# Cross-attention and a quantised FFN on one core: two stages with folded values against one unrolled pipeline without the fold

## What is computed

```python
def reference(x, ctx, proj_q, bias_q, proj_k, bias_k, proj_v, bias_v, w_out, w_gate, w_up, w_down):
    xn = layernorm(x)
    q = einsum('bnd,hdk->bhnk', xn, proj_q) + bias_q          # 16 heads of 64
    k = einsum('bnd,hdk->bhnk', ctx, proj_k) + bias_k
    v = einsum('bnd,hdv->bhnv', ctx, proj_v) + bias_v
    attn = softmax(einsum('bhqk,bhnk->bhqn', q, k) / 8)       # 154 columns a head
    hid = transpose(einsum('bhqn,bhnv->bhqv', attn, v))       # 1024 values a row
    x = x + hid @ w_out.T
    z = layernorm(x)
    h = silu(fp4_linear(z, w_gate)) * fp4_linear(z, w_up)     # 704 values a row
    return x + fp4_linear(h, w_down)

def fp4_quant_dequant(x):          # both operands of each fp4_linear, in blocks of 16
    scale = max(max(abs(block)) / 6, 1e-12)
    return grid_round(block / scale) * scale     # grid 0, .5, 1, 1.5, 2, 3, 4, 6 with sign
```

## Time and profile before

| | us |
|---|---|
| median of 3 runs | 482.89 (482.14 to 484.28) |
| span of the profiled execution, first to last instruction | 480.2 |
| TensorE matmul busy | 399.3 (83%) |
| VectorE busy | 410.6 (85%) |
| ScalarE busy | 283.6 (59%) |
| GpSimd busy | 232.4 (48%) |

### The profile page before, as it was taken

One profiled execution on the slowest core, in us unless ns is written; L12 is line 12 of the kernel. 1 busy time (PEld: TensorE's weight loads), 2 busy tenths in 40 slices (PEclk: granted clock), 3 DMA queues, 4 the chain that ended last, 5 costly groups with the idle time before them and its releaser, 6 DMA issues.

```text
span 480.2 us, 10222 instructions
## 1 busy us (share of the span) xinstructions
PE 399.3 (83%) x3581; PEld 308.9 (64%) x3581; DVE 410.6 (85%) x789; ACT 283.6 (59%) x862; POOL 232.4 (48%) x177
## 2 busy tenths in 40 slices
PE   1889769979989989799799899995687687696965
PEld 1668548858768768587687687883355464464753
DVE  2799886996987988979969879779989999989993
ACT  3597558757756677487577677755344554533641
POOL 7330133253352542542523523423877888768872
PEclk9999979999989999999999999998698998988999
DMA  7940000000000000000000000000000000000001
GB/s 244 315 175 1 2 0 1 2 2 1 1 0 0 0 0 0 0 0 0 0 0 0 1 0 1 1 1 1 1 0 1 23 11 11 22 11 11 23 13 54
DMA packets 8406, 11.18 MB, mean 23 GB/s; under 512 B 499, under 2 KB 6335, under 8 KB 8383
## 3 DMA queue, kind: packets, MB, share of 16 engines
q1 hardware_dynamic: 8383, 10.88, 7.1%
HBM read 8.78 MB, written 2.10 MB: 23 GB/s over the span
## 4 chain that ended last, share of the span: by engine, by line
DVE 52%; PE 29%; issue 9%; ACT 7%; DMA 1%; DVEq 1%; SPq 0%; POOLq 0%; POOL 0%; ACTq 0%
PE ps L356 8%; PE ps L357 7%; PE ps L358 7%; DVE arena L958 5%; DVE negmax L919 5%; PE ps L456 3%; DVE xn L869 3%; DVE arena L931 3%; DVE arena L910 3%; PE ps L448 3%; DVE vw L864 2%; DVE arena L1087 2%; DVE arena L1126 2%; DVE arena L975 2%; DVE arena L969 2%
## 5 line engine op out<-in xcount | busy, mean ns | idle before, releaser
L1178 POOL TENSOR_TENSOR arena<-arena,rinv 128x616 f32<-128x616 f32 x64 | 77.7, 1214 | 174.0 <-DVE rinv L927 174.0
L676 ACT ACTIVATE arena<-ps,ebias 128x154 f32<-128x154 f32 x256 | 96.2, 397 | 37.9 <-DVE ebias L922 37.5
L356 PE MATMUL ps<-vw,arena 128*128 128x256 f16 (+1 forms) x352 | 98.1, 279 | 24.0 <-DVE xs L939 10.7
L357 PE MATMUL ps<-vw,arena 128*128 128x256 f16 (+1 forms) x352 | 97.8, 278 | 0.0
L358 PE MATMUL ps<-vw,arena 128*128 128x256 f16 (+1 forms) x352 | 97.7, 278 | 0.0
L356 PE MATMUL ps<-arena,xnT_h 128*128 128x352 f16 x128 | 46.0, 359 | 27.0 <-DVE xnT_l L1009 25.6
L686 ACT ACTIVATE arena<-ps 128x512 f16<-128x512 f32 x80 | 48.4, 605 | 32.9 <-PE ps L456 32.3
L931 DVE TENSOR_TENSOR arena<-ps,arena 128x512 f16<-128x512 f32 x80 | 54.0, 675 | 8.4 <-ACT arena L686 7.8
L356 PEld LDWEIGHTS ps<-vw,arena 128*128 128x128 f16 x352 | 34.7, 99 | 33.8 <-DVE arena L931 20.3
L676 ACT ACTIVATION_READ_ACCUMULATOR arena<-ps,ebias 128x1 f32 x256 | 54.8, 214 | 0.0
L919 DVE TENSOR_REDUCE negmax<-ps 128x4 f32<-128x616 f32 x64 | 50.6, 790 | 2.9 <-PE ps L448 1.6
(11 more groups left out here) (136 smaller groups left out, 1033.1 us busy)
## 6 DMA issues: line engine op xcount, KB each, us to landing
out_dram<-arena SPq DMA_DIRECT2D x16, 128.0 KB, 1.7
xs<-in_x_dram SPq DMA_DIRECT2D x2, 896.0 KB, 10.1
arena<-in_L_xattn_w_out_dram SPq DMA_DIRECT2D x1, 1024.0 KB, 6.4
wffn<-in_L_ffn_w_down_dram SPq DMA_DIRECT2D x1, 704.0 KB, 8.0
wffn<-in_L_ffn_w_gate_dram SPq DMA_DIRECT2D x1, 640.0 KB, 11.0
wffn<-in_L_ffn_w_up_dram SPq DMA_DIRECT2D x1, 640.0 KB, 5.5
vw<-in_ctx_dram SPq DMA_DIRECT2D x1, 308.0 KB
xs<-in_x_dram SPq DMA_DIRECT2D x2, 128.0 KB, 5.0
```

The source lines that it names most:

```text
L356: pe.matmul(o, a_h, b_h, start=start, stop=False)
L357: pe.matmul(o, a_h, b_l, start=False, stop=False)
L676: last = act.activation(prob[:, s, h * L:(h + 1) * L], ps[:, 2 * (j % 2) + k % 2, (k // 2) * L:(k // 2 + 1) * L], ACT.Exp, bias=ebias[:, s ...
L1178: pool.tensor_tensor(v, v, rinv[:, s, 4 * j:4 * j + 4].unsqueeze(2).to_broadcast([P, 4, L]), ALU.mult).then_inc(normed, 1)
```

## The change

The change rewrites the kernel. Keys, queries, scores and the two-part products remain. What differs:

- There is no fold. Values stay as `v_h`, `v_l` (128 context rows) and the 26 rows left are kept for four heads together in `vl_h`, `vl_l`. For each unit of two tiles `mix` forms the transposed head outputs with 96 matmuls of 256 columns, whose outputs take 64 partitions each and alternate between the two halves; they are split into `hidT_h` and `hidT_l`, and `project` multiplies them by w_out (48 matmuls).
- Attention and FFN of a unit run in one pipeline of 11 steps of 8 slots, written out in full. In step s the scores, exponentials and transposes of unit s, the queries of unit s + 1, the head outputs of unit s - 1, the input quantiser and gate/up of unit s - 2, and the second hidden quantiser and down projection of unit s - 3 are issued. Units 0 to 7 exist.
- PSUM has three rings of two: banks 0 to 3 for scores and gate/up, banks 4, 5 for transposes, banks 6, 7 for queries, head outputs, projections and down.
- The quantiser has five passes: value (GpSimd), magnitude (one ScalarE `Abs`), two VectorE passes of `max` with add and subtract, scale (GpSimd).
- SiLU is `tanh` and a scaled copy on ScalarE, a VectorE pass with the up half, and a product on GpSimd (`gated`).
- The key is scaled beforehand, so that the row maximum is the bias of the exponential directly. The layernorm of x runs on ScalarE, the Newton steps of the inverse root on GpSimd in a chain of 14 small instructions; the result and x are added on VectorE.

The diff, cut to what the texts speak of (`unit(u)` is true for 0 to 7; `turned`, `grouped`, `s_bank`, `m_bank`, `t_bank` wait for and select a bank):

```diff
-            def fold(n):
...
+            def mix(u, j):
+                b = batch(2 * u)
+                pe.wait_ge(t_low, T_AT[("p", 2 * u + 1, 4)] + 1)
+                o = next_group(("pv", u, j))
+                for i in range(2):
+                    for n, (vh, vr, part) in enumerate(((v_h, vl_h, 0), (v_l, vl_l, 0), (v_h, vl_h, 1))):
+                        for r in range(2):
+                            h = 4 * j + 2 * i + r
+                            pe.matmul(o[r * DK:(r + 1) * DK, i * 256:(i + 1) * 256], vh[:, b, h * DK:(h + 1) * DK],
+                                      pT[:, u % 2, part, h], start=n == 0, stop=False)
+                        for r in range(2):
+                            last = pe.matmul(o[r * DK:(r + 1) * DK, i * 256:(i + 1) * 256], vr[:, b, j, 2 * i + r],
+                                             pT[:, u % 2, part, H + j], start=False, stop=n == 2)
+                last.then_inc(m_mm, 1)
...
+            def next_use(job):
...
+                if n >= 2:
+                    kind, i = S_ORDER[n - 2]
+                    if kind == "score":
+                        pe.wait_ge(exp_done, i + 1)
+                    else:
+                        pe.wait_ge(gu_act, i + 1)
+                        pe.wait_ge(gu_done, i + 1)
...
+            for step in range(STEPS):
+                for kk in range(8):
+                    k = 8 * step + kk
+                    if unit(step): score(k)
+                    if 0 <= k - 2 < 4 * TILES:
...
+                        turn_p(k - 2)
+                    if kk == 0:
+                        if unit(step - 2): project(step - 2, 1)
+                        if unit(step + 1): turn_x(step + 1)
+                        if unit(step - 3): turn_h(2 * (step - 3))
+                    if kk == 1:
+                        if unit(step - 3): down(2 * (step - 3))
+                        if unit(step + 1): query(step + 1, 0)
+                    if kk in (2, 3):
+                        if unit(step - 1): mix(step - 1, kk - 2)
+                        if kk == 3 and unit(step - 3): turn_h(2 * (step - 3) + 1)
+                        if unit(step + 1): query(step + 1, kk - 1)
+                    if kk == 4:
+                        if unit(step - 2): turn_xq(step - 2)
+                        if unit(step - 2): gate_up(4 * (step - 2))
+                        if unit(step - 3): down(2 * (step - 3) + 1)
+                    if kk in (5, 6):
+                        if unit(step - 1): mix(step - 1, kk - 3)
+                        if unit(step - 2): gate_up(4 * (step - 2) + kk - 4)
+                        if kk == 6 and unit(step + 1): query(step + 1, 3)
+                    if kk == 7:
+                        if unit(step - 2): gate_up(4 * (step - 2) + 3)
+                        if unit(step - 1): project(step - 1, 0)
...
+            def exps(k):
+                t, j = k // 4, k % 4
+                o = s_bank(("score", k))
+                act.wait_ge(max_done, k + 1)
...
+            def gate_act(g):
...
+                act.activation(act_h[t % 2][:, at], ps[:, o, 0:GU], ACT.Tanh, scale=0.5 / FS).then_inc(tanh_done, 1)
+                act.activation(gate[t % 2][:, at], ps[:, o, 0:GU], ACT.Copy, scale=0.5 / (FS * FS)).then_inc(gu_act, 1)
...
+                    if 0 <= k - 2 < 4 * TILES:
+                        p_high((k - 2) // 4, (k - 2) % 4)
...
+                    if unit(step): exps(k)
...
+                    if kk == 4 and unit(step - 2):
+                        xq_high(step - 2)
+                        gate_act(4 * (step - 2))
...
+                    if kk == 7 and unit(step - 2): gate_act(4 * (step - 2) + 3)
...
+                    if kk == 1 and unit(step - 3): magnitude(2 * (step - 3) + 1, hvalued, *tmp[1], hmagic)
+                    if kk == 7 and unit(step - 2): magnitude(2 * (step - 2), hvalued, *tmp[0], hmagic)
...
+            def to_grid(v, a, s, chain, done):
...
+                after(dve.scalar_tensor_tensor(v, a, 1.5 * GRID, v, ALU.max, ALU.add), s, chain)
+                dve.scalar_tensor_tensor(v, a, 1.5 * GRID, v, ALU.max, ALU.subtract).then_inc(done, 1)
...
+                    if unit(step): row_max(k)
...
+                    if kk == 0 and unit(step - 3): up_act(4 * (step - 3) + 3)
+                    if kk == 1 and unit(step - 2): add_attention(step - 2)
+                    if kk == 2 and unit(step + 1): q_low(step + 1, 0)
...
+                    if kk == 7 and unit(step + 1): q_low(step + 1, 3)
+                    if kk == 7 and unit(step - 2): up_act(4 * (step - 2) + 2)
...
+                    if 0 <= k - 2 < 4 * TILES:
+                        p_low((k - 2) // 4, (k - 2) % 4)
...
+                    if kk == 4 and unit(step - 2):
+                        xq_low(step - 2)
+                        up_act(4 * (step - 2))
+                    if kk in (5, 6) and unit(step - 1): hid_low(step - 1, kk - 3)
+                    if unit(step): inverse(k)
...
+                    if kk == 0 and unit(step - 3): scales_h(2 * (step - 3) + 1)
+                    if kk == 1 and unit(step - 3): grid_h(2 * (step - 3) + 1)
+                    if kk == 2 and unit(step - 2): scales_x(step - 2)
+                    if kk == 3 and unit(step - 2): grid_x(step - 2)
+                    if kk == 6 and unit(step - 2): scales_h(2 * (step - 2))
+                    if kk == 7 and unit(step - 2): grid_h(2 * (step - 2))
...
+            def gated(t):
+                pool.wait_ge(gu_done, 2 * t + 2)
+                pool.wait_ge(gu_act, 2 * t + 2)
+                pool.tensor_tensor(act_h[t % 2], act_h[t % 2], gate[t % 2], ALU.mult).then_inc(hid_ready, 1)
...
+                    if 0 <= k - 1 < 4 * TILES: norm(k - 1)
+                    if kk == 0:
+                        if unit(step - 3): round_h(2 * (step - 3))
+                        if unit(step - 3): gated(2 * (step - 3) + 1)
+                    if kk == 1:
+                        if unit(step - 3): value_h(2 * (step - 3) + 1)
+                        if unit(step - 2): norm_2(step - 2)
+                    if kk == 2 and unit(step - 3): round_h(2 * (step - 3) + 1)
+                    if kk == 3 and unit(step - 2):
+                        value_x(step - 2)
+                        round_x(step - 2)
+                    if kk == 6 and unit(step - 2):
+                        gated(2 * (step - 2))
+                        value_h(2 * (step - 2))
```

More of the change, by code:

```diff
@@ L66, in peeled @@
[L66 to L98 removed]
+WT_JOBS = [("w1", c, j) for c in range(KC) for j in range(0, W1T, 4)] + [("wd", 0, j) for j in range(0, FC, 2)]
@@ new lines, in scored_in @@
+def scored_in(step, kk):
+    if unit(step): yield ("score", 8 * step + kk)
+    if kk >= 4 and unit(step - 2): yield ("gu", 4 * (step - 2) + kk - 4)
+SLOTS = [(step, kk) for step in range(STEPS) for kk in range(8)]
+T_ORDER = [("bias",), ("ctx", 0), ("ctx", 1), ("x", 0)] + [j for s in SLOTS for j in turned_in(*s)]
+M_ORDER = [("q", 0, j) for j in range(QUADS)] + [j for s in SLOTS for j in mixed_in(*s)]
+S_ORDER = [j for s in SLOTS for j in scored_in(*s)]
+T_AT = {j: n for n, j in enumerate(T_ORDER)}
@@ new lines, in project @@
+            def project(u, s):
+                if s == 0:
+                    pe.wait_ge(m_done, M_AT[("pv", u, QUADS - 1)] + 1)
+                    o = next_group(("proj", u))
+                else:
+                    o = m_bank(("proj", u))
+                for p in range(PAIRS):
+                    last = three(o[:, s * D:(s + 1) * D], hidT_h[:, p, s * P:(s + 1) * P], hidT_l[:, p, s * P:(s + 1) * P],
+                                 wo_h[:, p], wo_l[:, p], p == 0, p == PAIRS - 1)
+                if s == 1: last.then_inc(m_mm, 1)
@@ L1150, in _ @@
-            steps(dve, ffn, first=2, last=STEPS - 2)
-            for t in range(2 * STEPS - 2, 2 * STEPS):
-                h_low(*step_of(t))
+                dve.wait_ge(wk_high, c + 1)
+                dve.scalar_tensor_tensor(heads_of(wk_l, c), by_chunk(raw_k)[:, c], WS, heads_of(wk_h, c),
+                                         ALU.mult, ALU.subtract).then_inc(wk_low, 1)
+            dve.wait_ge(ld_x0, 16)
+            norm_stats(0, 4)
+            norm_guess(0, 4)
+            x_low(0)
```

1690 lines of the change are left out of this document (780 added, 910 removed).

## The result

The changed kernel takes 575.5 us (median of 4 runs, 573.9 to 580.0) against 482.8 for the kernel before in the same comparison: a ratio of 1.191, 95% interval 1.184 to 1.197. The forecast was 545 us, slower. The direction and the likeliest case held, and the time lies in the range; the point was 30 us too low.

What follows compares the result with a forecast made beforehand. It took each slot's chain of in-order handovers to bound the kernel, not one engine's work. Set-up 46, steps 0 to 2 138, steps 3 to 6 219, step 7 51 and drain 92 made 546, given as 545 us; range 500 to 580.

Steps and rivals of the forecast that it cites:

- What bounds: Unit of two tiles: three engines have 36 to 39 us of work; whether in-order handovers hide is the question.
- Faster by overlap: Whole kernel: engines overlap as well as now, a unit takes 43.4 us, the whole 461; chance 0.15.
- the tie at 47: Middle of the loop: the two kernels tie when a unit takes near 47 us; chance 0.04.
- Slots: Middle step: the chains of slots 0 to 7, 4.9 to 8.4 us each, laid end to end make 54.7 us.
- a rival at 0.10: Whole kernel: unpaired `mix` adds 32 us and a fallen TensorE clock 14, together 591; chance 0.10.
- Step 2: Pipeline step with no final part and nine weight turns, priced at 51 us.
- The drain: Steps 8, 9 and 10, which empty the pipeline, priced at 39, 36 and 17 us.
- `mix` on halves: Head outputs on TensorE: matmuls alternating between array halves run in pairs, 5.2 us a unit.
- The other bound: Head outputs on TensorE: matmuls do not pair, 10.5 us a unit, about 4 us more a unit, 32 in all.
- Newton on GpSimd: Slot 1: 14 small instructions at 0.4 us each, 5.6 us, ending before `normal_x1` is due.
- Table loads: ScalarE: a load at each change between exponential and tanh adds 82 us, 627 in all; chance 0.03.
- What would show it: Changed profile: middle steps about 55 us, VectorE near 75% busy, waiting longest for tanh, magnitude and last transposes; one table load.

Runs made afterwards that it cites:

- the run that keeps the clock up: Changed kernel plus 22 unused matmuls in slot 4, 12 before the transposes and 10 behind them: 557.1 us, 1.151 against the kernel before.

## Why the prediction was right, and where it was short

**What bounds.** Right. The forecast said that three engines have 36 to 39 us of work in a unit and that handovers in order decide. Measured were 35.9 (VectorE), 32.8 (ScalarE) and 43.3 of latencies (TensorE) in 54.7. The added statistics passes, which cost nothing, and `down` moved, which gave 9 us without removing an instruction, show for slot 4 that the order and not the amount sets it; the other slots rest on their timelines. VectorE's sum of durations was 39.1, and the durations in that step add to 38.7; the busy time is 35.9, since each instruction's record overlaps the next by some 0.08 us. The forecast set a sum of durations against 45.0 of busy time; the sign of the result did not hang on it.

**Faster by overlap.** Fell. It needed slots 4, 7 and 0 under 6 us; they are 10.0, 7.4 and 8.5. The loop runs at 54.7, well above the tie at 47.

**Slots.** Five of eight within 0.5 us, and the sum exact, but by luck, because slots 1, 2, 3 and 7, priced 2.1 us too long together, cover slots 0 and 4, 2.1 too short. The failing step is the one that said of slot 4 "gate/up 3.85 to 5.65", at a full clock. Gate/up ends 7.3 us into the slot (346.41 - 339.11). The fallen clock stood in a rival at 0.10, priced 1.7 us a unit; the runs show 1.6 over the forecast, and 1.9 a step against the run that keeps the clock up. It is no rival but part of the kernel. The stall that makes it, 2.94 us, could be read off the forecast's own chain (nothing for TensorE until 1.1, little until 3.85), and the earlier trace rows had the halved rate behind a stall of 3.34. That should have been in the sum. The measured 575.5 is nearer to that rival's 591 than to 545; its other half, `mix` unpaired, did not happen, and step 2 and the drain, both priced too low, stand in its place. That the time lies in the range is in part luck too.

**Step 2.** The failing step with the largest part of the miss, 13 us. The forecast priced it "51", the step without its final part and with nine weight turns, as if a turn cost only its own instructions. It did not ask who frees the bank that a turned weight sits in, and when: VectorE, one slot later. The same question had been asked and answered for `project`, `turn_h` and the queries. Moving the low parts gave 8 of the 13 us; the other 5 have no experiment.

**The drain** was "39", "36" and "17", and took 41.4, 39.3 and 21.4, 10 us more. The last step's lines on TensorE and VectorE:

```profile
554.43 1.54 PE L500 MATMUL ps<-ident,ffn 128*128 128x128 f32 x6 [6.80 <-POOL ffn L1106]
...
564.87 1.53 PE L500 MATMUL ps<-ident,ffn 128*128 128x128 f32 x6 [3.70 <-POOL ffn L1106]
...
567.98 0.42 PE L320 MATMUL ps<-wdT,ffn 128*128 128x256 f16 x1
...
568.62 0.42 PE L320 MATMUL ps<-wdT,ffn 128*128 128x256 f16 x1
...
571.64 0.42 DVE L958 SCALAR_TENSOR_TENSOR rows<-ps,xs 128x256 f32<-128x256 f32 x1 [4.12 <-PE ps L320]
```

TensorE stands 6.80 us for the quantiser of the last hidden tile but one and 3.70 for that of the last; its passes follow one another with nothing to cover them. Then three matmuls of `down` take 0.64 us, where 0.33 is the full rate (three of the 0.109 in the earlier trace rows): with so little work the clock is down (0.64 over the step). The forecast had used middle-step durations for a drained pipeline. Steps 0 and 1, 5 us over together, have clocks of 0.80 and 0.84; that this is what made them longer is argued and was not tested.

The parts of the table add to 546 as forecast and 574 as measured. The forecast's last line (546, less one or two, plus 2.7) gives 547 and not the 545 it wrote; that slip adds two.

**`mix` on halves.** The bound taken was right: a pair in 0.11. The Trainium skill (TensorEngine Tiling (Array Packing), section Theoretical Speedup) has "Up to 2×" for it, and the trace agrees with the full factor of two, one pair in 0.11 us for one single matmul in 0.11. The forecast named the section Performance Considerations, which has the two-fold tiling and not the speed-up. The other bound was oversized: it charged all four slots (32 us), and 16 were measured.

**Newton on GpSimd.** Taken at 0.4 us an instruction, bounds 0.2 and 0.6. The trace has it just below the lower bound:

```profile
L1077 POOL TENSOR_TENSOR ln<-ln x30: 193/193/209, 14.8 to 524.5; 128x2 f32<-128x2 f32 x24, 128x4 f32<-128x4 f32 x3, 128x12 f32<-128x12 f32 x3
```

But the chain of 14 took 5.0 us (378.75 to 383.73 in the timeline), not far from the 5.6 of the forecast: its instructions start some 0.27 apart, and two of them, beside the two grid passes on VectorE, took 0.73 and 0.85. It is hidden, as said.

**Table loads.** The rival fell: one load in the whole kernel (L695 above, for two in the kernel before), with 256 exponentials and 32 tanh passes in turn. The Trainium skill (ScalarE: Activation LUTs, section Table sets: the hidden batching unit) puts both functions in one set; the trace agrees.

**What would show it.** Step about 55 us: 54.7. VectorE waits for tanh and magnitude: yes (36.7 and 27.6 us), but the 34.3 us before the low parts of the head outputs were not on the list. VectorE's share near 75%: 60% over the span and 66% in a middle step, which is less than said; the forecast's own 39.1 of 54.7 would be 71%.

**What stays open.** The change drops the fold and merges the stages at once, and no run separates the two, so how much of the 93 us is due to either is not shown. Open too are slot 0, still 8.5 us, and the reason for the first two steps. A merged pipeline with two or three hidden tiles in flight more, which might cover the handovers, was not tried.

## What to carry to other kernels

Where an in-order pipeline has several handovers in a slot, add up the chain of the slot, with the queue order and the owner of each bank; the busy times of the engines only say what is left to gain. Ask for each buffer filled in a special step who frees it and behind what that instruction stands. Price fill and drain as steps of their own, at the clock that the trace shows where TensorE has little to do, and try the parts of a rewrite one by one in the old kernel: here two of them were worth 18 us and the whole cost 93.

## What the runs showed of the hardware

- A VectorE pass with two fp32 inputs in SBUF (`scalar_tensor_tensor`, 704 values) takes 0.89 us alone. Begun 1.20 us before the end of a GpSimd pass over SBUF it took 1.96 and ended 0.76 after it; begun 0.14 before the GpSimd pass it kept its 0.89, and the GpSimd pass took 1.99 for 1.39.
- TensorE's granted clock fell to 0.50 (1.2 GHz) inside a stall of 2.94 us and stayed there for 6.8 us, through four transposes and all 12 gate/up matmuls, though these ran without a gap. With unused matmuls in the stall it stayed at 1.00, and the kernel was 18 us faster.
- Matmuls with outputs of 64 partitions that alternate between the two halves run two in 0.11 us at 256 columns each; in the other loop order they take twice that.
